# Chunk 0's x in 2 KB pieces ahead of W0, its units in pairs with four turns of the unit matrix before each pair of grams

## The chip, the cores and the metric

One Trainium2 chip, one of its cores. The time is that of the device, in microseconds, from the launch of the program to its end; lower is better. All data are fp32.

## The reference, cut to what matters

```
x = concat([bottom_mlp_output,                       # [2048, 128]
            pairs of einsum('bfd,bgd->bfg', b, b),   # b = bottom_output [2048, 27, 128]; 351 pairs f > g
            zeros], axis=1)                          # [2048, 480]
for w, b in ((w0, b0), (w1, b1), (w2, b2), (w3, b3)):    # 480 -> 1024 -> 1024 -> 512 -> 256
    x = relu(x @ w.T + b)
y = x @ w_out.T + b_out                              # [2048, 1]
```

## The kernel before, in words

The batch is cut into 8 chunks of 256 samples. A chunk has 16 **units** of 16 samples (4 groups of 4). For each sample the gram of its 27 rows of 128 is wanted. TensorE needs the rows turned (dimension in the partitions, tile `xt`), and makes the grams of a unit with 16 small matmuls (`gram`, L614 to 630; the profile counts each twice). A gram is copied from its bank of PSUM into `grams`. When all 16 units of a chunk are there, four DMAs write `grams` to `blocks` in DRAM (the **spill**, L389), and four more (the **gathers**, L394) read the pairs back with a pair in each partition, as the layers need them.

The four layers are products in three parts: a value is split into a high part and the rest (`w_hi`, `w_lo`), and high x high, low x high and high x low are summed. Chunk c has 408 such products of 128x128 by 256 columns (L671), 384 of them in layers 0 to 2. ScalarE drains each result with bias and relu (L763), VectorE and GpSimd split it (L856, L542). ScalarE also makes `w_hi` (L732), the high part of the pairs (L773) and copies grams (L748); VectorE makes `w_lo` (L835).

The order on every engine is written out by `first_steps` (the head, before chunk 0's products) and `chunk_steps`: while chunk c is multiplied, chunk c+1 is prepared at **hooks**, places in the run of products: one each 6 products in chunk 0 (`FIRST_HOOK`), each 36 later. At a hook stand two units (`unit_steps`: VectorE's transposes of the new pair, L844, then the grams of the pair before) and, in chunk 0, groups of four weight tiles that TensorE turns (L597) for layers 1 to 3. Two pairs of the chunk after next are raised ahead as well (`AHEAD`).

For chunk 0 the rows come whole (sample and feature in the partitions, `load_early`, L421 to 424, 448 pieces of 512 bytes for a unit), TensorE turns them with the unit matrix (`turn_early`, L602), ScalarE copies them into `xt` (L740), VectorE copies the gram (L850). Two banks take the turned rows. For all later chunks the rows come by 128-byte pieces in four DMAs a unit (`load_rows`, L426 to 442) into a ring of `ROWS_RING` = 4, and VectorE transposes them in blocks of 32.

Each of the engines works its list in order, and so does SyncE, which issues nearly all DMAs: x of chunk 0 units 0 to 8; the pairs' columns of W0; units 9 to 15; W0's other columns; mlp rows; biases; three of W1's four megabytes; half of chunk 0's spill and gathers (ScalarE issues the other half); W1's last megabyte; rows of chunk 1, units 0 to 3; W2 and W3. Then come the lists of the chunks:

```
sp.wait_ge(mlp_turned, c + 1)
load_mlp(c + 1)
start = isinstance(c, int) and c == 0
for u in range(ROWS_RING if start else ROWS_RING + AHEAD_UNITS, UNITS):
    load_rows(c + 1, u)
...
    for u in range(ROWS_RING):
        load_rows(c + 2, u)
spill(c + 1)
gather(c + 1)
```

A row DMA of unit u waits until the unit that lay in its slot has been transposed. The spill waits until the grams of its chunk are copied. ScalarE's first copy of a gram of the next chunk (`move_gram`, u = 0, L742 to 748) waits until that spill has landed, since `grams` is written again; for chunk 2's first gram this stands in chunk 0's list at product 324. W0's columns for the pairs are put into the gathers' order by GpSimd, 72 copies (L535, L536), and TensorE turns W0 afterwards.

Of the kernel before, what the change touches and what calls it, by code (L numbers as in the profile page):

```python
# [14 lines left out]
P = 128  # L15
# [5 lines left out]
GROUP = 4  # L21
# [6 lines left out]
ROWS_RING = 4  # L28
# [13 lines left out]
BEFORE_CHUNK, LATE_WEIGHTS = ORDER.index(W1_ALL[0]), ORDER.index(W2_ALL[0])  # L42
# [12 lines left out]
ACC_RING, GRAM_RING, TURN_RING = 3, 4, 2  # L55

XT_RING, XT_LAG, UNIT_LAG = 8, 2, 1
# [8 lines left out]
W1_EARLY, FIRST_UNIT, LATE_HOOK = 7, 6, 22  # L66
# [3 lines left out]
EARLY_SLOTS, SHORT_LAG = 8, 2  # L70
# [75 lines left out]
def first_steps():  # L146


    steps = []
    for u in range(UNITS + XT_LAG):  # L150
        if u < UNITS:
            steps.append(("turn", u))
        if 1 <= u <= SHORT_LAG:
            steps.append(("early", u - 1))
        elif u >= XT_LAG + SHORT_LAG:
            steps.append(("early", u - XT_LAG))
    steps += [("spill",), ("mlp",)] + [("weights", n) for n in range(BEFORE_CHUNK)]
    return steps + [("gather",)]


def first_hooks():
# [26 lines left out]
def chunk_steps(now, ahead, first):  # L188
# [47 lines left out]
def dlrm_program(nc, x, x_mlp, w0, b0, w1, b1, w2, b2, w3, b3, w_out, b_out, y):  # L236
    weights = [w0, w1, w2, w3]
    biases = [b0, b1, b2, b3]
    with ExitStack() as ctx:
# [20 lines left out]
        stage_pairs, = shared(("stage_pairs", [P, 8, PAIRS + 1]))  # L260
# [23 lines left out]
        w0_pairs_loaded = sem("w0_pairs_loaded")  # L284
        w0_in_order = sem("w0_in_order")
        w0_dense_loaded = sem("w0_dense_loaded")
# [36 lines left out]
        full_dims = [[DIM, FULL_ROWS], [GROUP * step_n, UNIT_GROUPS], [1, DIM]]  # L323
# [22 lines left out]
        def turned_bank(u):  # L346

            return side_ps if u % TURN_RING else acc[:, ACC_RING - 1]
# [22 lines left out]
        def samples(u):  # L371

            return xt[:, u % XT_RING].rearrange("p j (s f) -> p j s f", s=GROUP)[:, :, :, 0:FEATS]

        def gram_found(u):

            return gram_ps[:, u % GRAM_RING, 0:P].rearrange("p (j f) -> p j f", f=QUAD)[:, :, 0:FEATS]
# [18 lines left out]
        def early_rows_of(u):  # L396

            if u < EARLY_SLOTS:
                return early_rows[:, u]
            u -= EARLY_SLOTS  # L400
            return rows[:, u] if u < ROWS_RING else early_rows[:, u - ROWS_RING]

# [16 lines left out]
        def _(sp):  # L419
            def load_early(u):  # L420
                if u >= EARLY_SLOTS + ROWS_RING:  # L421

                    sp.wait_ge(turned, u - EARLY_SLOTS - ROWS_RING + 1)
# [98 lines left out]
        def _(pool):  # L522
# [9 lines left out]
            pool.wait_ge(w0_pairs_loaded, 16)  # L532
            ordered = raw_rows(0)[:, :, DIM:]
            for col, n, q, step in ROW_RUNS:
                nc.gpsimd.tensor_copy(ordered[:, :, q:q + (n - 1) * step + 1:step], stage_pairs[:, :, col:col + n])  # L535
            nc.gpsimd.tensor_copy(ordered[:, :, PAD_ROW:PAD_ROW + 1], stage_pairs[:, :, PAIRS:]).then_inc(w0_in_order, 1)  # L536
# [23 lines left out]
        def _(pe):  # L560
            def turn_weights(n):
# [5 lines left out]
                elif ring <= n < LATE_WEIGHTS:  # L567
# [11 lines left out]
                if g < W0_GROUPS:  # L579
                    layer, m, part = 0, g, 0  # L580
                    if g == 0:
                        pe.wait_ge(w0_in_order, 1)
                        pe.wait_ge(w0_dense_loaded, 16)
# [11 lines left out]
                for k in range(4):  # L595
                    at = (4 * part + k) * P
                    last = nc.tensor.transpose(bank[:, k * P:(k + 1) * P], src[:, at:at + P], ident[:])  # L597
# [15 lines left out]

            def gram(d, u):  # L614

# [3 lines left out]
                if isinstance(d, int) and d == 1 and u < GRAM_RING:  # L619
                    if u == 0:  # L620

                        pe.wait_ge(w_done, LATE_WEIGHTS)
                elif not (isinstance(d, int) and d == 0 and u < GRAM_RING):

                    pe.wait_ge(grams_done, d * UNITS + u + 1 - GRAM_RING)
                for j in range(UNIT_GROUPS):
                    for s in range(GROUP):
                        at = slice(QUAD * s, QUAD * (s + 1))
                        last = nc.tensor.matmul(gram_found(u)[at, j], xt[:, u % XT_RING, j, at], samples(u)[:, j, s],  # L629
# [316 lines left out]
```

## Time and profile before

| | us |
|---|---|
| median of 3 runs | 509.6 (508.92 to 510.27) |
| the profiled execution | 510.51 |
| its span, on which all rows are | 508.4 |
| TensorE busy | 485.8 |
| VectorE, ScalarE, GpSimd busy | 170.0, 161.6, 132.7 |

All places in time are microseconds from the start of the span. A row of the timeline gives the start, the length and the count of instructions that were merged; the length of a merged row ends with the last of them. PE is TensorE, DVE VectorE, ACT ScalarE, POOL GpSimd, and SPq the queue of SyncE that issues DMAs. Matmuls overlap, so that the distance of two starts tells what one costs. The granted clock of TensorE (PEclk) is 1.00 at 2.4 GHz and 0.50 at 1.2 GHz.

### The profile page before, as it was taken

The numbers are of one execution on the slowest core, as the hardware profiler recorded it, in microseconds if no ns is written. First come the engines' busy times: TensorE is split into PE (matmuls) and PEld (weight loads), VectorE is DVE, ScalarE is ACT, GpSimd is POOL, SyncE is SP. The second block draws the span as 40 slices with busy tenths as digits, with TensorE's granted clock in tenths as the row PEclk, the third lists the DMA queues.
The fourth block names the chain that finished last, engine by engine and source line by source line (L and its number), as shares of the span: only waits on it lengthen the run. The fifth ranks groups of instructions, "written<-read, shape, count | busy, mean of one in ns | idle before, by whom it ended". The sixth has DMA issues, their size and how long they took to land.

```text
span 508.4 us, 18568 instructions
## 1 busy us (share of the span) xinstructions
PE 485.8 (96%) x7595; PEld 467.0 (92%) x7595; DVE 170.0 (33%) x384; ACT 161.6 (32%) x380; POOL 132.7 (26%) x242
## 2 busy tenths in 40 slices
PE   6687967999999999999999999999999999999998
PEld 5576967999999999999999999999999999999997
DVE  1156624444322442134322442144322533131100
ACT  3255523424322342224222332224222432233112
POOL 1530311223312242123222232223222332124221
PEclk9679999999999999999999999999999999999999
DMA  8995876756666556744665556754565564300000
GB/s 219 246 314 143 231 130 100 117 106 123 101 99 121 103 92 108 133 90 77 100 101 113 102 90 95 139 98 68 91 106 125 84 95 72 71 30 2 1 0 1
DMA packets 281091, 53.88 MB, mean 106 GB/s; under 512 B 265126, under 2 KB 279230, under 8 KB 281022
## 3 DMA queue, kind: packets, MB, share of 16 engines
q1 hardware_dynamic: 279090, 52.22, 54.2%
q8 instruction: 60, 0.98, 0.8%
q10 hardware_dynamic: 1932, 0.61, 0.5%
q14 instruction: 9, 0.07, 0.1%
HBM read 45.71 MB, written 7.09 MB: 104 GB/s over the span
## 4 chain that ended last, share of the span: by engine, by line
PE 84%; SPq 8%; DMA 6%; DVE 1%; issue 1%; ACT 0%
PE acc L671 74%; PE gram_ps L629 8%; SPq L442 6%; DMA rows<-in_r_bottom_output_dram 4%; DMA blocks<-grams 2%; SPq L424 1%; PE side_ps L602 1%; PE side_ps L597 1%; PE acc L602 1%; PE side_ps L692 0%; DVE xt L844 0%; SPq L445 0%; SPq L394 0%; PE side_ps L645 0%; PE side_ps L686 0%
## 5 line engine op out<-in xcount | busy, mean ns | idle before, releaser
L671 PE MATMUL acc<-h_a,w_hi 128*128 128x256 f32 x1152 | 221.2, 287 | 0.0
L671 PEld LDWEIGHTS acc<-h_a,w_hi 128*128 128x128 f32 x1152 | 182.9, 191 | 2.2
L763 ACT ACTIVATE h_full<-acc,small_t 128x256 f32<-128x256 f32 x175 | 83.1, 475 | 264.7 <-PE acc L671 264.1
L671 PE MATMUL acc<-h_a,w_lo 128*128 128x256 f32 x576 | 158.6, 283 | 0.0
L542 POOL TENSOR_TENSOR h_a<-h_full,h_a 128x256 fp32r<-128x256 f32 x96 | 72.2, 752 | 175.2 <-DVE h_a L856 175.2
L671 PEld LDWEIGHTS acc<-h_a,w_lo 128*128 128x128 f32 x576 | 110.4, 192 | 0.0
L671 PE MATMUL acc<-x,w_hi 128*128 128x256 f32 x504 | 97.4, 286 | 1.1 <-ACT x L773 1.0
L671 PE MATMUL acc<-h_b,w_hi 128*128 128x256 f32 x512 | 96.8, 285 | 0.0
L542 POOL TENSOR_TENSOR h_b<-h_full,h_b 128x256 fp32r<-128x256 f32 x64 | 47.2, 739 | 179.3 <-DVE h_b L856 179.3
L671 PEld LDWEIGHTS acc<-x,w_hi 128*128 128x128 f32 x504 | 80.5, 191 | 2.3 <-ACT x L773 1.8
L671 PEld LDWEIGHTS acc<-h_b,w_hi 128*128 128x128 f32 x512 | 81.3, 192 | 0.2
L844 DVE STREAM_TRANSPOSE xt<-rows 128x512 f32<-128x512 f32 x112 | 73.5, 690 | 17.1 <-DMA rows<-in_r_bottom_output_dram 16.5
L671 PE MATMUL acc<-x,w_lo 128*128 128x256 f32 x252 | 70.4, 283 | 0.0
L671 PE MATMUL acc<-h_b,w_lo 128*128 128x256 f32 x256 | 70.0, 283 | 0.0
L856 DVE CAST h_a<-h_full 128x256 fp32r<-128x256 f32 x96 | 28.1, 293 | 123.8 <-ACT h_full L763 123.3
L856 DVE CAST h_b<-h_full 128x256 fp32r<-128x256 f32 x64 | 18.6, 292 | 142.3 <-ACT h_full L763 142.3
L629 PEld LDWEIGHTS gram_ps<-xt 128*32 128x32 f32 x4096 | 43.9, 114 | 15.8 <-issue 4.7
L629 PE MATMUL gram_ps<-xt 128*32 128x27 f32 x4096 | 51.8, 199 | 4.7 <-DVE xt L844 2.5
L671 PEld LDWEIGHTS acc<-h_b,w_lo 128*128 128x128 f32 x256 | 49.1, 192 | 0.0
L671 PEld LDWEIGHTS acc<-x,w_lo 128*128 128x128 f32 x252 | 48.3, 192 | 0.0
L748 ACT ACTIVATE grams<-gram_ps 128x108 f32<-128x108 f32 x112 | 36.0, 363 | 35.9 <-PE gram_ps L629 32.3
L597 PE MATMUL gram_ps<-ident,w_raw 128*128 128x128 f32 x96 | 14.1, 282 | 3.7 <-DVE w_lo L835 2.8
(54 smaller groups left out, 178.3 us busy)
## 6 DMA issues: line engine op xcount, KB each, us to landing
rows<-in_r_bottom_output_dram SPq DMA_DIRECT2D x444, 64.0 KB, 2.1
blocks<-grams SPq DMA_DIRECT2D x30, 216.0 KB, 4.0
w_raw<-in_L_rec_w_dram SPq DMA_DIRECT2D x6, 1024.0 KB, 7.5
early_rows<-in_r_bottom_output_dram SPq DMA_DIRECT2D x12, 224.0 KB, 5.9
stage_pairs<-in_L_rec_w_dram SPq DMA_DIRECT2D x1, 1408.0 KB, 11.7
w_raw<-in_L_rec_w_dram SPq DMA_DIRECT2D x2, 512.0 KB, 8.0
mlp_rows<-r_bottom_mlp_output_dram SPq DMA_DIRECT2D x8, 128.0 KB, 2.2
pairs<-blocks SPq DMA_DIRECT2D x8, 126.0 KB
```

Source lines behind the costliest of these rows:

```text
L424: sp.dma_start(early_rows_of(u)[0:FULL_ROWS], x_full[0, u]).then_inc(early_loaded[u], 16)
L442: sp.dma_start(dst, x_blocks[q][d, u]).then_inc(rows_loaded[r], 16)
L542: nc.gpsimd.tensor_tensor(h[:, m, 1, :], h_full[:, slot % 2, :], h[:, m, 0, :].bitcast(F32), ALU.subtract).then_inc(split_done, 1)
L597: last = nc.tensor.transpose(bank[:, k * P:(k + 1) * P], src[:, at:at + P], ident[:])
L602: last = nc.tensor.transpose(turned_bank(u)[:, j * GROUP_ROWS:(j + 1) * GROUP_ROWS], src[0:GROUP_ROWS, j, :], ident[0:GROUP_ROWS, 0:GROUP_ ...
L629: last = nc.tensor.matmul(gram_found(u)[at, j], xt[:, u % XT_RING, j, at], samples(u)[:, j, s], start=True, stop=True, tile_position=(0, Q ...
L671: last = nc.tensor.matmul(acc_slot(c, slot), weight(wp, layer, m, k), in_tile(layer, k, xp), start=(k == 0 and n == 0), stop=(k == K_TILES ...
L748: nc.scalar.activation(gram_place(u), gram_found(u), ACT.Copy).then_inc(grams_done, 1)
L763: nc.scalar.activation(h_full[:, slot % 2, :], acc_slot(c, slot), ACT.Relu, bias=small_t[:, slot:slot + 1]).then_inc(drained, 1)
L844: nc.vector.transpose(xt[:, u % XT_RING].rearrange("p j n -> p (j n)"), rows[:, r].rearrange("p j n -> p (j n)")).then_inc(xt_done, 1)
L856: nc.vector.tensor_copy(h[:, m, 0, :], h_full[:, slot % 2, :]).then_inc(high_done, 1)
```

## The change

- x of chunk 0: the partition now holds four rows that follow each other in DRAM, so that a unit is 112 pieces of 2 KB. All 16 units are issued first, W0 whole (one DMA, 480 columns) behind them. The turned rows come out in another order of columns, which ScalarE's copy (`early_xt`) puts right; `xt` of chunk 0 is now dense, with 27 columns a sample.
- The head goes by pairs of units: two turns, then the grams of the pair before. Ahead of each pair of grams `keep_clock` turns the unit matrix `FILL` = 4 times into the bank of the coming gram. The turned rows have four banks (`TURN_RING`), `xt` four slots instead of eight.
- The row ring has 8 slots instead of 4.
- W1 is issued after the gathers of chunk 0 have landed: its first megabyte, rows of units 0 to 3 of chunk 1, its other three megabytes, rows of units 4 to 7. All groups of W1, W2 and W3 are turned at hooks 2, 4, 6, ... of chunk 0; seven of W1's groups stood ahead of the pairs' products before.
- From chunk 1 on grams use two banks, and the weight groups two others.
- W0 is reordered by GpSimd and VectorE, half of the copies each. ScalarE issues its gathers before it copies weights.

```diff
-ROWS_RING = 4
+ROWS_RING = 8
...
-ACC_RING, GRAM_RING, TURN_RING = 3, 4, 2
-
-XT_RING, XT_LAG, UNIT_LAG = 8, 2, 1
+ACC_RING, GRAM_RING, TURN_RING, UNIT_BANKS = 3, 4, 4, 2
+
+XT_RING, UNIT_LAG = 4, 1
...
-W1_EARLY, FIRST_UNIT, LATE_HOOK = 7, 6, 22
+W1_HOOK, FIRST_UNIT = 2, 6
...
-EARLY_SLOTS, SHORT_LAG = 8, 2
+EARLY_SLOTS, FILL = 8, 4
...
-    for u in range(UNITS + XT_LAG):
+    for u in range(0, UNITS + 2, 2):
         if u < UNITS:
-            steps.append(("turn", u))
-        if 1 <= u <= SHORT_LAG:
-            steps.append(("early", u - 1))
-        elif u >= XT_LAG + SHORT_LAG:
-            steps.append(("early", u - XT_LAG))
-    steps += [("spill",), ("mlp",)] + [("weights", n) for n in range(BEFORE_CHUNK)]
-    return steps + [("gather",)]
+            steps += [("turn", u), ("turn", u + 1)]
+        if u:
+            steps += [("early", u - 2), ("early", u - 1)]
+    return steps + [("spill",), ("gather",), ("mlp",)] + [("weights", n) for n in range(BEFORE_CHUNK)]
...
-    for n in range(BEFORE_CHUNK + W1_EARLY, LATE_WEIGHTS):
-        hooks[n - BEFORE_CHUNK - W1_EARLY].append(("weights", n))
+    for n in range(BEFORE_CHUNK, W_GROUPS):
+        hooks[W1_HOOK + 2 * (n - BEFORE_CHUNK)].append(("weights", n))
...
-    for n in range(LATE_WEIGHTS, W_GROUPS):
-        hooks[LATE_HOOK + 3 * (n - LATE_WEIGHTS)].append(("weights", n))
...
-        steps += [("weights", BEFORE_CHUNK + n) for n in range(W1_EARLY)] + [("pairs", 0)]
+        steps += [("pairs", 0)]
...
-        full_dims = [[DIM, FULL_ROWS], [GROUP * step_n, UNIT_GROUPS], [1, DIM]]
+        full_dims = [[UNIT_GROUPS * DIM, FULL_ROWS], [DIM, UNIT_GROUPS], [1, DIM]]
...
-            return side_ps if u % TURN_RING else acc[:, ACC_RING - 1]
+            return side_ps if u % TURN_RING == ACC_RING else acc[:, u % TURN_RING]
...
-            return gram_ps[:, n % GRAM_RING, :] if n < LATE_WEIGHTS else side_ps[:, :]
+            return gram_ps[:, n % GRAM_RING if n < BEFORE_CHUNK else UNIT_BANKS + n % 2, :]
...
+        def early_xt(u):
+
+            return xt[:, u % XT_RING].rearrange("p j n -> p (j n)")[:, 0:UNIT_COLS].rearrange("p (q h) -> p q h", h=UNIT_GROUPS)
...
-            return turned_bank(u)[:, 0:UNIT_COLS].rearrange("p (j s f) -> p j s f", s=GROUP, f=FEATS)
+            return turned_bank(u)[:, 0:UNIT_COLS].rearrange("p (h q) -> p q h", h=UNIT_GROUPS)
...
-            for u in range(9):
+            for u in range(UNITS):
                 load_early(u)
-            sp.dma_start(stage_pairs[:, :, :], w0_rows[:, :, DIM:]).then_inc(w0_pairs_loaded, 16)
-            for u in range(9, UNITS):
-                load_early(u)
-            sp.dma_start(raw_rows(0)[:, :, 0:DIM], w0_rows[:, :, 0:DIM]).then_inc(w0_dense_loaded, 16)
+            sp.dma_start(stage_w0[:, :, :], w0_rows).then_inc(w0_loaded, 16)
...
-            for i in range(3):
-                load_weights(1, w1, 2 * i, 2 * i + 2, w1_loaded[i])
             spill(0, (0, 1))
             gather(0, PIECES[0::2])
-            load_weights(1, w1, 6, 8, w1_loaded[3])
-            for u in range(ROWS_RING):
+            for t in range(3):
+                sp.wait_ge(gathered[t], 16 * PIECES_OF[t])
+            load_weights(1, w1, 0, 2, w1_loaded[0])
+            for u in range(ROWS_RING // 2):
+                load_rows(1, u)
+            for i in range(1, 4):
+                load_weights(1, w1, 2 * i, 2 * i + 2, w1_loaded[i])
+            for u in range(ROWS_RING // 2, ROWS_RING):
                 load_rows(1, u)
...
-            for col, n, q, step in ROW_RUNS:
+            for col, n, q, step in ROW_RUNS[0::2]:
...
-                    pe.wait_ge(w_done, n)
-                    pe.wait_ge(drained, slot_count(0, ACC_RING))
+                    pe.wait_ge(w_done, n - 1)
...
+            def keep_clock(u):
+
+                for n in range(FILL):
+                    nc.tensor.transpose(gram_ps[:, u % GRAM_RING, (n % 4) * P:(n % 4 + 1) * P], ident[:], ident[:])
+
             def gram(d, u):
+
+                if isinstance(d, int) and d == 0:
+                    if u >= GRAM_RING:
+
+                        pe.wait_ge(grams_done, u + 1 - GRAM_RING)
+                    if u % 2 == 0:
+                        keep_clock(u)
...
+            def order_w0():
+
+                dve.wait_ge(w0_loaded, 16)
+                ordered = raw_rows(0)[:, :, DIM:]
+                for col, n, q, step in ROW_RUNS[1::2]:
+                    last = nc.vector.tensor_copy(ordered[:, :, q:q + (n - 1) * step + 1:step], stage_w0[:, :, DIM + col:DIM + col + n])
+                last.then_inc(w0_in_order, 1)
...
                 if step[0] == "early":
                     early_move(step[1])
+                elif step[0] == "spill":
+                    order_w0()
```

## Rows read from the trace of the kernel before

**Rows 1.** The page: busy time, share of the span and instructions

```profile
PE 485.8 (96%) x7595; PEld 467.0 (92%) x7595; DVE 170.0 (33%) x384; ACT 161.6 (32%) x380; POOL 132.7 (26%) x242
```

**Rows 2.** Stretches: length, TensorE busy (matmuls), granted clock, DMA share, GB/s

```profile
4.20:11.00 6.80, 6.77 (x121) 1.00 1.11 245
11.00:17.80 6.80, 3.40 (x141) 0.99 1.13 300
17.80:24.70 6.90, 5.95 (x144) 0.50 0.97 229
24.70:31.50 6.80, 6.80 (x187) 0.51 0.98 371
```

**Rows 3.** Timeline of the head: start, length, instruction, idle time before it

```profile
4.23 0.95 PE L602 MATMUL acc<-ident,early_rows 108*128 108x108 f32 x4 [4.23 <-DMA early_rows<-in_r_bottom_output_dram]
...
11.38 0.59 PE L602 MATMUL acc<-ident,early_rows 108*128 108x108 f32 x4
...
12.29 0.59 PE L602 MATMUL side_ps<-ident,early_rows 108*128 108x108 f32 x4
...
18.18 11.43 POOL L535 COPY w_raw<-stage_pairs 128x8 f32<-128x8 f32 x71 [15.70 <-DMA stage_pairs<-in_L_rec_w_dram]
...
23.24 0.98 PE L602 MATMUL acc<-ident,early_rows 108*128 108x108 f32 x4
...
24.73 0.98 PE L602 MATMUL side_ps<-ident,early_rows 108*128 108x108 f32 x4
...
33.14 4.45 ACT L732 ACTIVATE w_hi<-gram_ps 128x512 fp32r<-128x512 f32 x8
...
38.60 1.91 PE L597 MATMUL gram_ps<-ident,w_raw 128*128 128x128 f32 x16
...
45.59 0.38 PE L671 MATMUL acc<-x,w_hi 128*128 128x256 f32 x1 [0.99 <-ACT x L773]
```

**Rows 4.** Timeline of SyncE's queue (58.32 twice: to 67.2, and whole)

```profile
30.57 2.29 SPq L389 DMA_DIRECT2D blocks<-grams  x2
39.41 1.67 SPq L394 DMA_DIRECT2D pairs<-blocks  x2
41.12 0.45 SPq L445 DMA_DIRECT2D w_raw<-in_L_rec_w_dram  x1
41.62 14.37 SPq L442 DMA_DIRECT2D rows<-in_r_bottom_output_dram  x16
56.03 1.51 SPq L445 DMA_DIRECT2D w_raw<-in_L_rec_w_dram  x3
...
58.32 9.02 SPq L442 DMA_DIRECT2D rows<-in_r_bottom_output_dram  x6
...
58.32 46.02 SPq L442 DMA_DIRECT2D rows<-in_r_bottom_output_dram  x64
104.38 3.45 SPq L389 DMA_DIRECT2D blocks<-grams  x4
112.21 3.02 SPq L394 DMA_DIRECT2D pairs<-blocks  x4
```

**Rows 5.** Waits (us, times, longest): SyncE 58 to 104.3; VectorE, TensorE 45.5 to 117.7

```profile
SPq L442 <- DVE xt L844: 1.7, 5, 0.5
...
DVE xt L844 <- DMA rows<-in_r_bottom_output_dram: 15.5, 7, 5.9
...
PE side_ps L597 <- DVE w_lo L835: 4.2, 2, 2.5
PE gram_ps L629 <- DVE xt L844: 2.5, 2, 1.6
```

**Rows 6.** Timeline of ScalarE and TensorE where chunk 1 begins

```profile
112.27 0.55 ACT L748 ACTIVATE grams<-gram_ps 128x108 f32<-128x108 f32 x2 [3.67 <-DMA blocks<-grams]
...
117.53 0.28 PE L671 MATMUL acc<-x,w_hi 128*128 128x256 f32 x1
...
117.72 0.42 ACT L773 ACTIVATE x<-pairs 128x256 fp32r<-128x256 f32 x1 [0.19 <-DMA pairs<-blocks]
```

More of the change, by code:

```diff
@@ L41 @@
 ORDER = W0_ALL + SMALL + W1_ALL + W2_ALL + W3_ALL
-BEFORE_CHUNK, LATE_WEIGHTS = ORDER.index(W1_ALL[0]), ORDER.index(W2_ALL[0])
+BEFORE_CHUNK = ORDER.index(W1_ALL[0])
 HIGH, LOW, ALL = (0, 1), (2,), (0, 1, 2)
@@ L258, in dlrm_program @@
         h_full = sb("h_full", [P, 2, CHUNK])
-        stage_pairs, = shared(("stage_pairs", [P, 8, PAIRS + 1]))
+        stage_w0, = shared(("stage_w0", [P, 8, LAYERS[0][0]]))
         _, weighted = shared(("weighted_gap", [P, 5 * 2 * CHUNK]), ("weighted", [P, CHUNK]))
@@ L283, in dlrm_program @@
         small_loaded = sem("small_loaded")
-        w0_pairs_loaded = sem("w0_pairs_loaded")
+        w0_loaded = sem("w0_loaded")
         w0_in_order = sem("w0_in_order")
-        w0_dense_loaded = sem("w0_dense_loaded")
         w1_loaded = [sem(f"w1_loaded{i}") for i in range(4)]
@@ L369, in raw_rows, with samples, gram_found @@
             return w_raw[:, TILE0[n] * P:TILE0[n + 1] * P].rearrange("p (m k) -> p m k", k=k)
[L371 to L377, printed above, removed]
+        def samples(d, u, j, s):
+            if isinstance(d, int) and d == 0:
+                at = GROUP_ROWS * j + FEATS * s
+                return xt[:, u % XT_RING].rearrange("p j n -> p (j n)")[:, at:at + QUAD]
+            return xt[:, u % XT_RING, j, QUAD * s:QUAD * (s + 1)]
+        def early_xt(u):
+            return xt[:, u % XT_RING].rearrange("p j n -> p (j n)")[:, 0:UNIT_COLS].rearrange("p (q h) -> p q h", h=UNIT_GROUPS)
+        def gram_found(d, u):
+            bank = u % GRAM_RING if isinstance(d, int) and d == 0 else u % UNIT_BANKS
+            return gram_ps[:, bank, 0:P].rearrange("p (j f) -> p j f", f=QUAD)[:, :, 0:FEATS]
         def gram_place(u):
@@ L400, in early_rows_of @@
             u -= EARLY_SLOTS
-            return rows[:, u] if u < ROWS_RING else early_rows[:, u - ROWS_RING]
+            return rows[:, u]
         def tile_of_group(g):
@@ L420, in load_early @@
             def load_early(u):
-                if u >= EARLY_SLOTS + ROWS_RING:
-                    sp.wait_ge(turned, u - EARLY_SLOTS - ROWS_RING + 1)
                 sp.dma_start(early_rows_of(u)[0:FULL_ROWS], x_full[0, u]).then_inc(early_loaded[u], 16)
@@ L530, in _ @@
                 nc.gpsimd.memset(raw_rows(0)[:, :, DIM + t * P + n:DIM + (t + 1) * P], 0.0)
[L532 removed]
+            pool.wait_ge(w0_loaded, 16)
             ordered = raw_rows(0)[:, :, DIM:]
[L534 to L536 removed]
+            for col, n, q, step in ROW_RUNS[0::2]:
+                nc.gpsimd.tensor_copy(ordered[:, :, q:q + (n - 1) * step + 1:step], stage_w0[:, :, DIM + col:DIM + col + n])
+            nc.gpsimd.tensor_copy(ordered[:, :, PAD_ROW:PAD_ROW + 1], stage_w0[:, :, DIM + PAIRS:]).then_inc(w0_in_order, 1)
             def split_low(c, layer, m):
@@ L566, in turn_weights @@
                     pe.wait_ge(grams_done, UNITS + 1 - ring + n)
-                elif ring <= n < LATE_WEIGHTS:
+                elif n < BEFORE_CHUNK:
                     pe.wait_ge(w_done, n + 1 - ring)
                 else:
-                    pe.wait_ge(w_done, n)
-                    pe.wait_ge(drained, slot_count(0, ACC_RING))
+                    pe.wait_ge(w_done, n - 1)
                 if g == W0_GROUPS:
@@ L581, in turn_weights @@
                     if g == 0:
-                        pe.wait_ge(w0_in_order, 1)
-                        pe.wait_ge(w0_dense_loaded, 16)
+                        pe.wait_ge(w0_in_order, 2)
+                        pe.wait_ge(w0_loaded, 16)
                 else:
@@ L596, in turn_weights @@
                     at = (4 * part + k) * P
-                    last = nc.tensor.transpose(bank[:, k * P:(k + 1) * P], src[:, at:at + P], ident[:])
+                    cols_k = stage_w0[:, m, 0:DIM] if layer == 0 and k == 0 else src[:, at:at + P]
+                    last = nc.tensor.transpose(bank[:, k * P:(k + 1) * P], cols_k, ident[:])
                 last.then_inc(w_turned, 1)
@@ L612, in turn_early @@
                 turn_rows(u, early_rows_of(u))
+            def keep_clock(u):
+                for n in range(FILL):
+                    nc.tensor.transpose(gram_ps[:, u % GRAM_RING, (n % 4) * P:(n % 4 + 1) * P], ident[:], ident[:])
             def gram(d, u):
+                if isinstance(d, int) and d == 0:
+                    if u >= GRAM_RING:
+                        pe.wait_ge(grams_done, u + 1 - GRAM_RING)
+                    if u % 2 == 0:
+                        keep_clock(u)
+                elif isinstance(d, int) and d == 1 and u < UNIT_BANKS:
+                    if u == 0:
+                        pe.wait_ge(w_done, BEFORE_CHUNK)
+                else:
+                    pe.wait_ge(grams_done, d * UNITS + u + 1 - UNIT_BANKS)
                 pe.wait_ge(xt_done, d * UNITS + u + 1)
@@ L618, in gram @@
                     pe.wait_ge(xt_zeroed, 1)
[L619 to L625, printed above, removed]
                 for j in range(UNIT_GROUPS):
                     for s in range(GROUP):
-                        at = slice(QUAD * s, QUAD * (s + 1))
-                        last = nc.tensor.matmul(gram_found(u)[at, j], xt[:, u % XT_RING, j, at], samples(u)[:, j, s],
+                        at, one = slice(QUAD * s, QUAD * (s + 1)), samples(d, u, j, s)
+                        last = nc.tensor.matmul(gram_found(d, u)[at, j], one, one[:, 0:FEATS],
                                                 start=True, stop=True, tile_position=(0, QUAD * s))
```

8 lines of the change are left out of this document (4 added, 4 removed).

## The prediction

> **What bounds the kernel now.** The page comes first: TensorE is busy for 485.8 us, 96% of the span [rows 1], so what is to be won lies where it is not. The table of stretches [rows 2] shows where that is: 3.40 of 6.80 us between 11.0 and 17.8, and half speed from there to 31.5. That is the head, chunk 0's units and W0, before the products of chunk 0 can start. The timeline of the head [rows 3] shows a unit (turn plus gram) every 0.91 us at 2.4 GHz (11.38 to 12.29) and every 1.49 us at 1.2 GHz (23.24 to 24.73).
>
> After the head one must look at SyncE's queue [rows 4]. It issues everything in written order: chunk 0's spill at 30.57, gathers at 39.41, then from 41.12 to 104.38 W1's last megabyte, 16 row transfers, three issues of W2 and W3, the mlp rows and 64 more row transfers, and only then chunk 1's spill. In 58 to 104 us it waited 1.7 us in all [rows 5]: it is saturated by the issuing itself. Between 45.5 and 117.7 VectorE stood 15.5 us waiting for rows, and TensorE 4.2 and 2.5 us for VectorE [rows 5].
>
> Last, what hangs on chunk 1's spill [rows 6]. ScalarE stood 3.67 us until it had landed (112.2), and converted the third tile of pairs at 117.72, while TensorE's first product of chunk 1 is at 117.53. So chunk 1 starts 13.2 us after its spill is issued (104.38 to 117.53), and the pairs came with hardly any margin. Chunk 0's end is set jointly by TensorE's work and by SyncE's queue. From 117.5 on TensorE is nearly always busy; the sum is therefore made at chunk 1's start.
>
> **The head.** All of x comes before W0, and TensorE finds units 8 to 15 landed: in the 512-byte pieces of before, 245 GB/s were moved in 4.2 to 11.0, and 371 GB/s when W1's longer pieces ran in 24.7 to 31.5 [rows 2]. One unit is 229 KB, 0.94 us at the first rate, 0.62 at the second; both are less than what a unit costs TensorE with its fill (below), or about equal, so TensorE sets the pace. Fill: 16 turns of 128x128 took 1.91 us [rows 3], 0.12 each, so four are 0.48 us at 2.4 GHz and 0.95 at 1.2. A pair of units costs 2x0.91+0.48 = 2.30 us, or 2x1.49+0.95 = 3.93 us. The first turn is at 4.23. The matmuls of 4.2 to 11.0 ran at the lower level too: the column says 1.00, but the first unit's four turns took 0.95 us as those at 23.24 did (0.98), and 0.59 at 11.38. TensorE had been busy for 6.77 of those 6.80 us. I take the same rise at 11.0: 6.8/3.93 = 1.7 pairs until then, 6.3 pairs x 2.30 = 14.4 us after it, 25.4, and 0.4 for the last copy: spill at 25.8 instead of 30.57. Bounds: 23.0 if the clock is up from the start (8x2.30), 28.6 if it rises only at 17.8, 36.0 if never (8x3.93).
>
> The spill took 8.84 us (30.57 to 39.41) beside three megabytes of W1, and 7.83 us from one queue in chunk 1 (104.38 to 112.21) [rows 4]. Now W1 is gone from beside it and two queues issue: 7.6, between 5.9 (a third less) and 8.8. It lands at 33.4. The gathers: ScalarE read the first tile 3.05 us after their issue and the last 5.5 us after it in chunk 1, beside row transfers [rows 4, 6]; alone and over two queues I take 3.5 (3.0 to 4.5): 36.9.
>
> W0 lands behind x (5.6 MB at 300 to 371 GB/s, 16 to 20 us). Its reordering, 71 copies in 11.43 us on GpSimd [rows 3], becomes 35 or 36 of them there (5.8 us, done at some 26) and the rest on VectorE behind its last gram copy. Those 35 copies aren't in the trace: at GpSimd's 0.16 us each they end at 31.5, under the spill's landing. Cost nothing; were the spill's cover gone it would be up to 5.7 us. ScalarE now waits for the spill, issues its gathers (some 1.9 us), then copies the mlp tile and nine weight groups, 4.45 us for eight [rows 3]: products with pairs can start at some 40.3 instead of 45.59 [rows 3]. W1's seven groups, turned while TensorE had nothing else, now lie among the products: 7x0.48 = 3.3 us. If TensorE were the only limit, that would be the whole of it.
>
> **The queue.** SyncE now waits until the gathers have landed (36.9) and goes on where it went on at 41.12 before: 4.2 us earlier. What stands ahead of chunk 1's spill grows by two things.
> - Sixteen row transfers more. With a ring of eight, units 0 to 7 of chunk 2 are written ahead of chunk 1's spill, where units 0 to 3 were; each is four issues. The 64 transfers of 58.32 to 104.34 took 46.02 us, 5.3 of it for W2 and W3 (next point) and 1.7 waiting: 0.61 us each. 16x0.61 = 9.8 us (16x0.53 = 8.5 at the least; 16x0.90 = 14.4 as in the 14.37 us from 41.62).
> - Three megabytes of W1, issued in the head before, now behind it. Right after W2 and W3 (2.5 MB) six row transfers took 9.02 us where 3.7 is normal [rows 4]: 5.3 us, 2.1 per MB; with 0.5 for each issue 3x2.6 = 7.9 us (1.5, the issues alone, to 9).
> The ring of eight takes away the 1.7 us of waiting. From 41.12 to 104.38 it was 63.3 us; now 63.3+9.8+7.9-1.7 = 79.3. So chunk 1's spill is issued at 36.9+79.3 = 116.2 instead of 104.38, 11.8 us later. The rows of chunk 1's own units gain nothing either: their queue starts 4.2 us earlier and has 7.9 us more of W1 in it.
>
> Does TensorE get there sooner? Products from 40.3; at the tenth hook (60 products on) it needs W1's second megabyte, issued behind 16 row transfers at some 37.4+14.4 = 51.8 and landed near 56, while TensorE is there near 49.5 (60x0.12 and four groups of 0.48 after 40.3): a stop of 6 to 7 us. Units come at the pace of their rows. At product 324 ScalarE meets the gram of chunk 2 that waits for the spill, and everything it drains afterwards stands behind that wait, where it stood 3.67 us before. TensorE can fill three accumulators, then it stops, until 116.2+7.8. From there the order is that of before, so chunk 1 starts at 116.2+13.2 = 129.4, 11.8 us after 117.5.
>
> In the later chunks the same 64 row transfers lie between two spills as before: 7.83 until the gathers' issue, 3.02 for that [rows 4] and 64x0.61 = 39 make 50 us, and seven chunks share 508.4-117.5, 56 us each. So the queue doesn't lose more there, and what chunk 0 lost isn't made good. The rings of two gram banks and four xt buffers there cost nothing: a pair is raised while the pair before it is multiplied; with that cover gone, a copy of 0.3 us per unit.
>
> **Sum.** Profiled execution 510.5 us (span 508.4 and 2.1 around it) + 11.8 = 522.3; the median of the runs is 0.9 under the profiled one: 509.6+11.8 = 521.4, and I say 521. The ends: head 5 us less or 5 more, queue 7.8 less (71.5) or 7 more. The forecast's own range is 513 to 528.
>
> **A rule on the clock.** The rows show the clock at 0.50 from 17.8 to 31.5, with TensorE busy 5.95 of 6.90 us and then 6.80 of 6.80 [rows 2]; at 38.60 turns of 0.12 us show it up again [rows 3], and it was up at 11.0 after 24 turns and three units' grams. So a stretch full of turns was followed by a rise, and I count the fill as activity. The Trainium skill, TensorE: Matmul & The Clock Gate, Part 4 (PE-mode transpose), says that work in transpose mode does not count as busy for the clock gate. By that rule the fill only costs, which is rival 2; by the rows it helps.
>
> **Rivals.**
> 1. TensorE, not SyncE's queue, sets chunk 1's start; the weights hide behind row issues. It would decide if chunk 1's spill were issued within 67.5 us of 36.9, that is by 104.4, against 79.3 in my sum. Then: 5.3 us earlier start, 3.3 back for W1's groups, 7.7 us of stops gone (4.2 for w_lo, 2.5 for xt [rows 5] and 1.0 for the pairs at 45.59 [rows 3]), 6.5 for the new stop at W1: 3.2 us faster, 506.4; without that stop 500. For it: the head gains for certain, and in 11.0 to 31.5 transfers and weights ran side by side at 229 to 371 GB/s [rows 2]. Against it: 1.7 us of waiting in 46 us of issuing. Chance 0.18.
> 2. The clock stays at 1.2 GHz in the head, since turns don't count or since four are too few: spill at 36.0, 10.2 us later than forecast, 531. Against it: 6.77 of 6.80 us busy sufficed at 11.0, and pairs leave fewer gaps. Chance 0.08.
> 3. The change doesn't do what it says in one respect: W1's price is hidden but not the rows': 79.3-6.4 = 72.9, 514. Chance 0.04; that all of it cancels to within 0.3%, 0.04.
>
> **How the numbers follow.** Forecast 0.66, and 0.12 for the other two slower ones: slower 0.78, the same 0.04 (0.3%, about 1.5 us, is what a measurement of this kernel can tell), faster 0.18. The range from 512 to 529 takes in the forecast's own, rival 3 and half-way cases to rival 2; it leaves out rival 1 and most of rival 2.
>
> **What would show it.** Right: chunk 0's first spill near 26; the granted clock up from about 11 to at least 26; in SyncE's queue 96 row transfers between W1's first megabyte and the spill of chunk 1, that spill at 112 to 120; ScalarE's wait for it many us instead of 3.67; TensorE idle before chunk 1's first product, near 129; a stop at W1's second megabyte near 50. Wrong: the spill of chunk 1 at or before 104, row transfers issued at 0.53 each with the weights in between costing nothing, or a head at half speed.

## The result and the profile after

The changed kernel takes 523.74 us (median of 4 runs, 522.55 to 527.75) against 509.26 for the kernel before on the same chip: ratio 1.0304, 95% interval 1.0264 to 1.0343, slower by 14.5 us. The forecast was 521 (11.8 us slower), with a range of 512 to 529. The profiled execution is the slowest of the four, 527.75 us with a span of 526.0, so its places in time are some 4 us late against the median.

The page, busy time (against [rows 1]):

```profile
PE 492.1 (94%) x7627; PEld 475.4 (90%) x7627; DVE 172.1 (33%) x419; ACT 160.8 (31%) x380; POOL 126.8 (24%) x207
```

TensorE is busy 6.3 us more in a span that is 17.6 us longer (the rows of the fill, the extra turns of the unit matrix, are 6.1 us); the rest is standing still. The timeline of SyncE's queue, which answers to [rows 4]:

```profile
33.07 1.39 SPq L391 DMA_DIRECT2D blocks<-grams  x2
39.88 1.65 SPq L396 DMA_DIRECT2D pairs<-blocks  x2
45.38 0.41 SPq L444 DMA_DIRECT2D w_raw<-in_L_rec_w_dram  x1
45.83 11.09 SPq L441 DMA_DIRECT2D rows<-in_r_bottom_output_dram  x16
56.96 1.51 SPq L444 DMA_DIRECT2D w_raw<-in_L_rec_w_dram  x3
58.52 16.23 SPq L441 DMA_DIRECT2D rows<-in_r_bottom_output_dram  x16
74.79 1.51 SPq L444 DMA_DIRECT2D w_raw<-in_L_rec_w_dram  x3
76.35 0.98 SPq L462 DMA_DIRECT2D mlp_rows<-r_bottom_mlp_output_dram  x1
77.37 44.70 SPq L441 DMA_DIRECT2D rows<-in_r_bottom_output_dram  x64
122.12 3.49 SPq L391 DMA_DIRECT2D blocks<-grams  x4
```

All 96 row transfers stand between W1's first megabyte and the spill of chunk 1. That spill is issued at 122.12, where it was 104.38. The queue waited only 1.4 us for free slots on the way. The chain of work that ended last runs over this queue up to the spill, so chunk 1 hangs on it. The timelines of ScalarE and TensorE there (against [rows 6]):

```profile
128.93 0.53 ACT L760 ACTIVATE grams<-gram_ps 128x108 f32<-128x108 f32 x2 [12.20 <-DMA blocks<-grams]
...
130.09 0.58 PE L683 MATMUL acc<-h_a,w_hi 128*128 128x256 f32 x1 [6.67 <-DVE h_a L876]
...
134.52 0.41 PE L683 MATMUL acc<-x,w_hi 128*128 128x256 f32 x1
```

What TensorE waited for in 45 to 135 (us, times, longest):

```profile
PE acc L683 <- DVE h_a L876: 6.7, 1, 6.7
PE gram_ps L597 <- DMA w_raw<-in_L_rec_w_dram: 4.4, 1, 4.4
PE gram_ps L641 <- DVE xt L856: 1.4, 1, 1.4
```

ScalarE stood 12.20 us (3.67 before) at the gram that may only be moved when the spill has landed. TensorE filled its accumulators, reached layer 3 and stopped for 6.67 us; the name in the row is VectorE's, which waited for ScalarE's drains. The 4.4 us are the stop at W1's second megabyte. Chunk 1 begins at 134.52, 17.0 us after 117.53. From there to the end it is 391.5 us (390.9 before), and 390.7 to 391.4 in every version below: whatever a version gains or loses is settled before chunk 1 starts.

The stretches of the head, with their granted clock (against [rows 2]):

```profile
4.20:11.00 6.80, 5.30 (x85) 1.00 0.99 262
11.00:17.80 6.80, 4.73 (x136) 1.00 1.06 270
17.80:24.70 6.90, 5.49 (x133) 0.75 0.63 236
24.70:31.50 6.80, 5.90 (x252) 1.00 0.03 6
```

The clock is at 2.4 GHz for 17 of the head's 29 us: the turns and grams up to 13.0 still took as long as those at 1.2 GHz (0.98 us for four turns, whatever the column says), and the column shows 0.50 from 19.8 to 23.2. TensorE has gaps at either level. The first spill comes at 33.07, not at 25.8, and even 2.5 us after that of the kernel before. And x in 2 KB pieces moved at 262 GB/s in the first stretch, against 245 at 512 bytes.

One execution is a coarse measure of a head. e1_spill_ahead, below, has the same head instruction for instruction, and there the first spill came 2.2 us earlier:

```profile
30.87 1.68 SPq L391 DMA_DIRECT2D blocks<-grams  x2
```

So a difference of some 2 us between the heads of two single executions shows nothing.

### The profile page after: what moved, and what is told of

The parts are those of the page before. It is cut to its first block, busy times and chain, and to the rows that moved or that the text cites. A ratio compares the mean times of both kernels' runs of the same rounds, so it can differ in the third digit from the quotient of the medians.

```text
span 526.0 us, 18616 instructions
## 1 busy us (share of the span) xinstructions
PE 492.1 (94%) x7627; PEld 475.4 (90%) x7627; DVE 172.1 (33%) x419; ACT 160.8 (31%) x380; POOL 126.8 (24%) x207
## 4 chain that ended last, share of the span: by engine, by line
PE 81%; SPq 10%; DMA 5%; issue 2%; DVE 1%; ACT 0%; ACTq 0%; DVEq 0%
PE acc L683 69%; SPq L441 9%; PE gram_ps L641 8%; DMA blocks<-grams 2%; DMA early_rows<-in_r_bottom_output_dram 1%; DMA rows<-in_r_bottom_output_dram 1%; PE acc L602 1%; PE gram_ps L617 1%; DMA pairs<-blocks 1%; PE gram_ps L597 1%; SPq L444 1%; SPq L391 1%; PE side_ps L602 0%; PE side_ps L704 0%; DVE xt L856 0%
## 5 line engine op out<-in xcount | busy, mean ns | idle before, releaser
L683 PE MATMUL acc<-h_a,w_hi 128*128 128x256 f32 x1152 | 224.5, 289 | 6.7 <-DVE h_a L876 6.7
L683 PEld LDWEIGHTS acc<-h_a,w_hi 128*128 128x128 f32 x1152 | 184.9, 193 | 8.9 <-DVE h_a L876 6.9
L542 POOL TENSOR_TENSOR h_b<-h_full,h_b 128x256 fp32r<-128x256 f32 x64 | 47.1, 737 | 178.2 <-DVE h_b L876 178.2
L683 PEld LDWEIGHTS acc<-x,w_hi 128*128 128x128 f32 x504 | 82.0, 195 | 0.6
L641 PEld LDWEIGHTS gram_ps<-xt 128*32 128x32 f32 x4096 | 42.9, 112 | 15.7 <-issue 6.0
L641 PE MATMUL gram_ps<-xt 128*32 128x27 f32 x4096 | 50.1, 197 | 5.9 <-issue 4.5
L760 ACT ACTIVATE grams<-gram_ps 128x108 f32<-128x108 f32 x112 | 35.9, 363 | 38.2 <-PE gram_ps L641 25.8
L847 DVE TENSOR_TENSOR w_lo<-gram_ps,w_hi 128x512 fp32r<-128x512 f32 x34 | 23.0, 686 | 23.6 <-ACT w_hi L744 23.6
## 6 DMA issues: line engine op xcount, KB each, us to landing
stage_w<-in_L_rec_w_dram SPq DMA_DIRECT2D x1, 1920.0 KB, 14.5
```

The source lines that it names most:

```text
L542: nc.gpsimd.tensor_tensor(h[:, m, 1, :], h_full[:, slot % 2, :], h[:, m, 0, :].bitcast(F32), ALU.subtract).then_inc(split_done, 1)
L641: last = nc.tensor.matmul(gram_found(d, u)[at, j], one, one[:, 0:FEATS], start=True, stop=True, tile_position=(0, QUAD * s))
L683: last = nc.tensor.matmul(acc_slot(c, slot), weight(wp, layer, m, k), in_tile(layer, k, xp), start=(k == 0 and n == 0), stop=(k == K_TILES ...
L760: nc.scalar.activation(gram_place(u), gram_found(d, u), ACT.Copy).then_inc(grams_done, 1)
L847: last = nc.vector.tensor_tensor(w_lo[:, a:b], bank, w_hi[:, a:b].bitcast(F32), ALU.subtract)
```

## The experiments

All are timed beside the kernel before, which had 508.7 to 508.9 us as the median of those comparisons. The sizes below are differences of medians to it: +14.5 for the changed kernel.

### Which part of the queue's order costs what

**e1_spill_ahead.**

```diff
                 if more:
-                    for u in range(ROWS_RING):
+                    for u in range(ROWS_RING // 2):
                         load_rows(c + 2, u)
                 spill(c + 1)
                 gather(c + 1)
                 if more:
-                    for u in range(ROWS_RING, ROWS_RING + AHEAD_UNITS):
+                    for u in range(ROWS_RING // 2, ROWS_RING + AHEAD_UNITS):
```

> The changed kernel with one thing moved: in each chunk's list on SyncE the spill and the gathers of the next chunk stand behind rows of units 0 to 3 of the chunk after it, as before the change, and units 4 to 7 come after them. Theory (SyncE's queue sets chunk 1's start): 16 row transfers at 0.54 to 0.61 us leave the way of the spill, which is issued 9 to 10 us earlier, near 113; chunk 1's first product comes near 126, where TensorE's own work ends (it stood at 123.3 with 24 products to go), and its clock has no long stop to fall in: 9 us faster than the changed kernel, 514 to 516. Rival (TensorE's work or the rows of chunk 1 set it): within 2 us of the changed kernel.

517.55 us, ratio 1.0180 (1.0137 to 1.0222): +8.8. SyncE's queue there:

```profile
75.58 34.99 SPq L441 DMA_DIRECT2D rows<-in_r_bottom_output_dram  x48
110.62 3.38 SPq L391 DMA_DIRECT2D blocks<-grams  x4
```

The spill comes at 110.6 and chunk 1 starts at 124.2. From W1's first issue (43.33) to the spill it is 67.3 us, 9.4 less than the changed kernel's 76.7, so the 16 transfers cost the queue what was expected. The gain of the whole is 6 us rather than 9, and the chain that ended last shows why. The last transfer on it is one of chunk 1's rows, landed at 87.2; after that it stays nearly all with TensorE until chunk 1 begins, and the spill isn't on it:

```profile
84.96 2.28 DMA rows<-in_r_bottom_output_dram
...
116.11 9.94 PE acc L683 x80
```

With the queue this much shorter, TensorE's own work ends last. The profiled execution of the changed kernel, from which the 9 was read, was also 4 us over its median. The rival (within 2 us) is out.

**e2_w1_in_head.**

```diff
+            for i in range(3):
+                load_weights(1, w1, 2 * i, 2 * i + 2, w1_loaded[i])
             spill(0, (0, 1))
...
-            load_weights(1, w1, 0, 2, w1_loaded[0])
-            for u in range(ROWS_RING // 2):
-                load_rows(1, u)
-            for i in range(1, 4):
-                load_weights(1, w1, 2 * i, 2 * i + 2, w1_loaded[i])
-            for u in range(ROWS_RING // 2, ROWS_RING):
+            load_weights(1, w1, 6, 8, w1_loaded[3])
+            for u in range(ROWS_RING):
                 load_rows(1, u)
```

> The changed kernel with three megabytes of W1 issued in the head again, the last one after the gathers; all else as changed. Theory (queue): 3 MB at 2.1 us and three issues of 0.5 leave the way of chunk 1's spill: issued 7 to 8 us earlier, near 114.5; less what the spill of chunk 0 loses beside W1 in the head (up to 1.3 us). TensorE's stop of 4.4 us for W1's second megabyte goes. In all 6 to 8 us faster than the changed kernel, 516 to 518. Rival (the price of the weights is hidden behind the issuing of rows, only the 16 row transfers count): within 2 us.

520.52 us, ratio 1.0240 (1.0197 to 1.0283): +11.8, so 3 us gained of 6 to 8; the interval overlaps that of the changed kernel slightly.

```profile
34.91 1.93 SPq L391 DMA_DIRECT2D blocks<-grams  x2
...
46.80 0.39 SPq L444 DMA_DIRECT2D w_raw<-in_L_rec_w_dram  x1
47.24 20.80 SPq L441 DMA_DIRECT2D rows<-in_r_bottom_output_dram  x32
...
114.31 3.41 SPq L391 DMA_DIRECT2D blocks<-grams  x4
```

From W1's first issue behind the gathers to chunk 1's spill it is 67.5 us, 9.2 less than the changed kernel's 76.7; 7.9 was the price. But the first spill is at 34.9, later than in either execution of the changed head (33.07 and 30.87). What W1 gives the queue it takes in part in the head, not by slowing the spill (34.91 to 41.16) but earlier: TensorE's unexplained stops were 6.5 us in all, 5.2 in the changed kernel and 3.8 in e1 (see below).

**e3_both** is e1 and e2 together.

> Both edits at once: the order of SyncE's queue is that of before again, with x ahead of W0, 2 KB pieces, the ring of eight and the fill left in. Theory: the two parts add up, chunk 1's spill is issued near 106 and chunk 1 starts at 119 to 120: 14 to 15.5 us faster than the changed kernel, 508.5 to 511, level with the kernel before. Rival (the slow head with its late first spill and the hooks carry a part of the loss of their own): 513 or more.

512.87 us, ratio 1.0078 (1.0053 to 1.0103): +4.1. The two parts give 5.7 and 2.7 apart and 10.4 together, of 14.5: within the noise of each, about 2 us, they add up. The queue's order is more than two thirds of the loss. The expectation of a level result was wrong by 2 to 4 us, as its rival said; what is left isn't in the queue's order, and the head is where it was looked for. From W1's last megabyte to the spill:

```profile
47.25 0.40 SPq L444 DMA_DIRECT2D w_raw<-in_L_rec_w_dram  x1
...
106.59 3.41 SPq L391 DMA_DIRECT2D blocks<-grams  x4
```

With e1 and e2 beside it, the queue's 76.7 us can be told apart: 59.3 us for what stood in it before, 8.2 (e2 less e3) to 9.4 (changed kernel less e1) for the 16 transfers, 8.0 (e1 less e3) to 9.2 (changed kernel less e2) for the three megabytes of W1.

**e6_before_ring8** puts the same cause into the kernel before. To make room it also halves the slots of `xt`.

```diff
-ROWS_RING = 4
+ROWS_RING = 8
...
-XT_RING, XT_LAG, UNIT_LAG = 8, 2, 1
+XT_RING, XT_LAG, UNIT_LAG = 4, 2, 1
```

> The kernel before with a ring of eight row slots and four xt slots (for room), nothing else. Its list on SyncE then has units 0 to 7 of chunk 2 ahead of chunk 1's spill instead of 0 to 3. Theory: 16 row transfers at 0.61 us, less 1.7 us of waits that the ring takes away: the spill of chunk 1 at 111.5 to 113 instead of 104.4, and the whole 7 to 8.5 us slower, 516 to 517.5. Rival (the ring costs nothing by itself, it was the late head that made the queue late): within 1.5 us of the kernel before.

517.76 us, ratio 1.0171 (1.0151 to 1.0191): +8.9. Its SyncE queue:

```profile
41.28 22.82 SPq L442 DMA_DIRECT2D rows<-in_r_bottom_output_dram  x32
64.14 2.73 SPq L445 DMA_DIRECT2D w_raw<-in_L_rec_w_dram  x3
...
67.89 43.95 SPq L442 DMA_DIRECT2D rows<-in_r_bottom_output_dram  x64
111.89 3.43 SPq L389 DMA_DIRECT2D blocks<-grams  x4
```

ScalarE's timeline where chunk 1 begins:

```profile
118.61 0.53 ACT L748 ACTIVATE grams<-gram_ps 128x108 f32<-128x108 f32 x2 [11.10 <-DMA blocks<-grams]
```

With the head of before and W1 where it was, the larger ring makes chunk 1's spill 7.5 us late and the kernel 8.9 us slower. Sixteen more transfers took 22.82-14.37 = 8.5 us [rows 4], 0.53 each. The fewer slots of `xt` weren't timed alone, but nothing points at them: the queue got to W1's last megabyte 0.35 us earlier than before, and from there to the spill it waited 1.4 us for VectorE, against 1.7. This is the clearest of the runs: a deeper ring is a longer list ahead of the spill, because the list was written ring by ring.

### The head: fill, clock, and stops that nothing explains

**e4_no_fill** sets FILL to 0. 

> The changed kernel without the fill (none instead of four turns of the unit matrix ahead of a pair of grams; no result depends on them). Theory (the fill counts as activity and holds the clock, but the head's lateness is TensorE standing still for nothing that the profile shows, some 5 us): without it the granted clock stays at 0.50 for longer in the first 33 us, eight fills of 0.48 to 0.95 us fall away, and the two about cancel: chunk 0's spill at 31 to 35, the whole within 2 us of the changed kernel. Rival 1 (turns don't count for the clock, so the fill is only work): clock as with it, spill 4 to 6 us earlier, near 28, and as much faster. Rival 2 (the fill is what holds the clock, and all hangs on it): spill at 37 or later, 4 us slower.

521.49 us, ratio 1.0250 (1.0199 to 1.0302): +12.8, by the medians 2 us faster than with the fill, though the intervals overlap, and the first spill at 30.08 (33.07 and 30.87 with it). Stretches of the head:

```profile
11.00:17.80 6.80, 3.74 (x121) 0.84 1.06 288
17.80:24.70 6.90, 5.60 (x147) 0.50 0.55 200
24.70:31.50 6.80, 5.29 (x206) 0.66 0.02 5
```

The clock falls at 15.7 and is back at 29.3; with the fill it was at 0.50 from 19.8 to 23.2, and in e1, with the same head, from 16.9 to 23.7. So the stretch at half speed was 13.7 us without the fill and 3.4 or 6.8 with it. The fill shortens it, and still doesn't pay.

**e11_fill_doubled** sets FILL to 8. 

> The changed kernel with eight turns instead of four. Theory (once the clock is up a fill is only work): 32 turns more at 0.12 to 0.24 us, 4 to 7 us of TensorE in the head, of which the clock gives back at most the 3.4 us of the stretch at 0.50; chunk 0's spill near 36 and the whole 1 to 4 us slower than the changed kernel. Rival (more activity pays): the granted clock stays up through the whole head and the whole is no slower.

526.42 us, ratio 1.0347 (1.0307 to 1.0386): +17.7. The first spill was at 33.10, not near 36. The clock was at 0.50 for 6.8 us, no less than with four turns in e1, and at 1.00 from 24.7 on. The whole is 2.7 us slower than the changed kernel, inside what was expected of it. Zero, four and eight turns give +12.8, +14.5 and +17.7: each four cost some 2 to 3 us. The intervals of neighbours overlap, those of zero and eight don't. Where the eight lose theirs isn't settled, since only one execution of each was profiled.

**The stops.** In the changed kernel's chain of waits through the head, in order of time:

```profile
15.18 0.55 PE gram_ps L641 x42
15.73 2.67 issue
18.41 0.33 PE gram_ps L641 x16
...
23.82 0.80 issue
...
27.96 0.75 issue
...
31.35 1.00 issue
```

"issue" is time in which the engine waited for nothing that the profile shows. These four come in the middle of a run of grams or turns, 5.2 us in all, and the long one is the one that falls while x and W0 are being moved; the three short ones fall when the transfers have ended (0.03 DMA share in 24.7 to 31.5). The page lists a DMA queue of its own for instructions, 60 packets; in the trace packets of 16 KB start at 15.7, 22.2, 25.9 and 29.8, each 2.4 to 2.8 us ahead of a stop's end. The packet itself takes 1.0 to 1.3 us each time, also at the long stop: what differs is how late it starts. That made the theory: TensorE runs out of instructions, and their load stands behind the data in the same 16 DMA engines. The stops also belong to places in the program and not to times. The first leaves 16 records of grams in the changed kernel, e1, e2, e3, e7 and e8 alike, at 16.3 to 18.4; the third leaves two turns in all of these but e1.

**e5_x_gated** keeps few transfers in flight.

```diff
             def load_early(u):
+                if u >= 4:
+                    sp.wait_ge(turned, u - 3)
```

> The changed kernel, in which SyncE issues chunk 0's unit u from 4 on only when unit u-4 has been turned, so that few row transfers are in flight in the head; W0 then comes behind them, later. Looked at is only the head. Theory (the stops of TensorE after which the profile names nothing, 2.7 us at 15.7 and 0.8 to 1.0 us later, are loads of TensorE's own instructions, which queue behind the data in the same DMA engines): with the engines nearly free the first of them shrinks from 2.7 to at most 1.2 us. Rival (they have nothing to do with the data in flight): it stays at 2.5 to 3.3 us. The whole is no faster than the changed kernel, since W0 is later.

One execution, 522.11 us. The rows of TensorE's timeline in the head that end such a stop:

```profile
18.09 0.61 PE L643 MATMUL gram_ps<-xt 128*32 128x27 f32 x43 [0.65 <-issue]
...
23.52 0.49 PE L604 MATMUL side_ps<-ident,rows 108*128 108x108 f32 x2 [2.05 <-issue]
...
27.82 0.31 PE L643 MATMUL gram_ps<-xt 128*32 128x27 f32 x11 [0.26 <-issue]
```

No stop is left in 14 to 17 us, and the second, at 17.4, is 0.65 us. The stop of 2.05 us isn't the first one moved: it stands at the place of the third, with two turns left, which was 0.75 us in the changed kernel with the engines idle and now has W0 under way (DMA share 1.00 in 21.4 to 23.5). Where W1 is in the head, the same place cost 2.9 to 3.2 us in e2, e3, e7 and e8:

```profile
30.43 0.34 PE L600 MATMUL side_ps<-ident,rows 108*128 108x108 f32 x2 [3.23 <-issue]
```

The first spill is at 28.54, 2.3 to 4.5 us earlier than in the two executions of the changed head, though nothing was taken from TensorE's work. So the first and the third stop were long with data in flight and short or gone without it. The second hardly moved: 0.80 us in the changed kernel, and 1.0 to 1.1 in e2, e3, e7 and e8 with the engines full (DMA share 1.02 to 1.06 in 21 to 24). And e11, with more turns between the grams, had none after the first. That the stops are instruction loads is read from the packets' times and from these fixed places, and wasn't tested by itself. It fits the late heads of e2 and e3.

### Towards a version that beats both

**e7_no_gather_wait** is e3 without SyncE's wait for chunk 0's gathers.

```diff
-            for t in range(3):
-                sp.wait_ge(gathered[t], 16 * PIECES_OF[t])
```

> As e3_both (the order of the queue as before the change), and SyncE doesn't wait until chunk 0's gathers have landed before it goes on. That wait was 5.6 us less 1.7 of issuing. Theory: SyncE goes on 3.9 us earlier, near 43.3; the gathers share the engines with W1's last megabyte, but ScalarE reads the pairs only at 49.3; chunk 1's spill near 103 instead of 106.6: 3 to 4 us faster than e3_both where the queue sets the end, 509 to 510. Rival (TensorE, whose products with pairs start at 50.3 there, sets it by now): within 1.5 us of e3_both.

512.42 us, ratio 1.0070 (1.0048 to 1.0092): +3.6, so nothing beyond the noise against e3. The spill of chunk 1 came at 103.90 instead of 106.59, but ScalarE no longer waited for it (3.8 us in e3), and from 60 us on the chain that ended last is nearly all TensorE's: the rival.

**e8_w1_early** adds to e7 the order of before on ScalarE and TensorE.

```diff
-    return steps + [("spill",), ("gather",), ("mlp",)] + [("weights", n) for n in range(BEFORE_CHUNK)]
+    return steps + [("spill",), ("mlp",)] + [("weights", n) for n in range(BEFORE_CHUNK)] + [("gather",)]
...
-        steps += [("pairs", 0)]
+        steps += [("weights", BEFORE_CHUNK + n) for n in range(W1_EARLY)] + [("pairs", 0)]
```

> As e7_no_gather_wait, and ScalarE issues its gathers behind the nine weight groups again, and seven groups of W1 are turned ahead of the pairs' products, as before the change. TensorE and ScalarE work while the spill and the gathers are under way: products with pairs near 47 instead of 50.3 and 3.3 us less of weight turns among them. Theory: TensorE's part gets 5 to 6 us shorter; with the queue's 3.9 us from e7_no_gather_wait, 505 to 508, the first version that is faster than the kernel before. Rival (ScalarE's half of the gathers comes late, or the queue alone sets the end): no faster than e7_no_gather_wait.

511.34 us, ratio 1.0052 (1.0027 to 1.0077): +2.5. Too much was hoped for: 5 to 6 us of TensorE's part gave one, inside the noise. Chunk 1's spill now waited 2.9 us for its grams, so the queue was ahead of TensorE.

**e9_w1_early_no_fill** is e8 with FILL at 0. 

> As e8_w1_early without the fill. There chunk 1's spill waited 2.9 us for its grams, so TensorE's side sets the end by now. Theory (the fill buys clock but costs what it buys; without it, in e4_no_fill, the first spill came 3 us earlier and the whole was 2.2 us faster): spill of chunk 0 at 30.5 to 32 instead of 33.5, 1 to 3 us faster than e8_w1_early, 508.5 to 510.5. Rival (the fill is worth its time, e4_no_fill was a lucky phase of the clock): 511 or more.

509.00 us, ratio 0.9998 (0.9977 to 1.0018), level with the kernel before, 2.3 us faster than e8, with intervals apart: this is the pair that shows that the fill costs, and by about what the medians gave in e4. TensorE stood 7.8 us in three such stops in its head, with 2 KB pieces, W0 and W1 all issued at once:

```profile
PE gram_ps L637 <- issue: 7.8, 3, 4.0
```

**e10_also_gated** is e9 with unit u of chunk 0, from 5 on, issued when u-4 units have been turned (by the edit; that is unit u-5). 

> As e9_w1_early_no_fill, and unit u of chunk 0 from 5 on is issued only when unit u-4 has been turned. Theory (instruction loads queue behind data): TensorE's stop near 14 goes from some 3 us to under 1; but W0 and three megabytes of W1 now run in 18 to 30 us and the later stops stand in their way, and W0 lands near 27 instead of 23, so that GpSimd's half of it is ready near 33. Spill of chunk 0 near 29, W0 turned from 33 on; 507.5 to 510. Rival (W0's lateness costs what the head gains): within 1 us of e9_w1_early_no_fill or slower.

507.36 us, ratio 0.9968 (0.9946 to 0.9989; 12 runs against 23): 1.4 us faster than the kernel before, the only version that beats both. Its stops in the head:

```profile
17.71 0.40 PE L639 MATMUL gram_ps<-xt 128*32 128x27 f32 x25 [0.90 <-issue]
...
24.64 1.65 PE L639 MATMUL gram_ps<-xt 128*32 128x27 f32 x108 [3.75 <-issue]
```

The first is short, the second, with W0 and W1 in flight behind the units, is as long as ever. The first spill is at 26.72. Against e9 alone the intervals overlap, so that the gate's own worth isn't settled.

## Why the prediction was right, and where it was not

- **SyncE's queue sets chunk 1's start: right.** The forecast was 79.3 us from W1's first issue to chunk 1's spill; it was 76.7. The spill came at 122.12, outside the 112 to 120 that was to show it, because the queue started late. Of the terms, 16 row transfers, 9.8 us less 1.7, were 8.2 to 9.4, and three megabytes of W1, 7.9, were 8.0 to 9.2. The 63.3 us taken over from before were 59.3 in e3, 3.9 too many; why the same list went faster there isn't shown. The 1.7 us of waiting that the ring was to take away were still 1.4.
- **Chunk 1 follows its spill by 13.2 us: right.** It was 12.4, with ScalarE's wait in the place and TensorE's stop for its drains as described. That TensorE's clock would fall in that stop (0.51 in 129 to 136) wasn't foreseen.
- **TensorE's stop at W1's second megabyte: right**, 4.4 us for 6 to 7, and covered in the changed kernel as said. In e1, with the queue shorter, it is on the chain.
- **The head: wrong by 7.3 us** (33.07 for 25.8). The step that failed is "TensorE sets the pace", with 2.30 us for each pair. It had two faults. The kernel before showed a stop in the midst of a unit's grams:

```profile
15.49 0.26 PE L629 MATMUL gram_ps<-xt 128*32 128x27 f32 x6 [2.25 <-issue]
```

  The sum has no term for it. It isn't a wait for x; x ahead of W0 doesn't remove it, and such stops recur, 5.2 us in all. And x at 2 KB was priced at up to 371 GB/s, a rate of W1's 4 KB pieces; at 262 GB/s TensorE stood 1.5 us for units 2 and 3. The rest is the clock, at 1.2 GHz until 13.0 and in 19.8 to 23.2. At 7.3 us the miss is larger than the 5 that the sum allowed the head.
- **The wait for the gathers** was 5.5 us for 3.5 (39.88 to 45.38), over its upper bound of 4.5; the spill 6.8 for 7.6. The pairs, which were to be ready for products at 40.3, were converted by ScalarE from 47.6 on.
- **The errors cancelled in part, and that is luck.** Head and gathers were 8.5 us too early, the queue 2.6 and the last step 0.8 too long. The sum was 11.8; measured were 14.5 by medians and 17.0 at chunk 1's start in the profiled execution. The cause that was forecast holds; that the number lies within 3 us owes something to errors of opposite sign.
- **The clock.** The prediction counted turns as activity, and the changed kernel shows it more plainly than the fill does. From 33.4 the clock was at 0.50, TensorE did nothing but 16 turns of weights from 36.3 to 39.9, and at 40.3 the clock rose:

```profile
33.50:40.00 6.50, 3.64 (x16) 0.50 0.68 140
40.50:43.50 3.00, 0.00 (x1) 1.00 0.30 80
```

  The Trainium skill, TensorE: Matmul & The Clock Gate, Part 4, says that transposes don't count as busy; these rows speak against it. But the conclusion drawn, that a fill which holds the clock helps, was wrong: by e8 and e9 it costs 2 us. What was also not foreseen is that TensorE, idle while the spill and the gathers are under way, would have its clock at 0.50 in 33.4 to 40.3 and in 43.7 to 47.1, where it was at 1.00 before.
- **Rival 1 (TensorE sets the end)** is out for the changed kernel, and true of e7 to e10, whose queue is short enough. Rival 2 (half speed in the whole head) is out by the 1.00 in 13.0 to 19.8 and from 23.2 on, though its other half, a fill that only costs, came true by another way than turns that don't count. Rival 3 (W1's price hidden) is out by e2's 9.2 us.

## What to carry to other kernels

In a queue that issues in written order, look for what the next stage waits for (here a spill of 3.5 us) and count what stands ahead of it; a ring made deeper moves its prefetches ahead of it too, and here the deeper ring cost 9 us in a kernel that was otherwise as before (e6). Once such a queue is short enough, the next limit, here TensorE, takes over, and further cuts give less than they free (e1, e7). A stop with nothing behind it in the middle of a run of instructions wasn't a wait for x here, and at two places of the program it was longer with more data in flight. Work that only keeps the clock up must be weighed against the time at the lower clock that it saves: here four turns a pair took 6.1 us of TensorE, shortened the stretch at half speed from 13.7 us to 3.4 or 6.8, and lost.

## What the runs showed of the hardware

- In 4.2 to 11.0, with x under way in 229 KB transfers, 2 KB pieces moved at 262 GB/s in the changed kernel and at 272 to 304 in the eight others that issue all of x at once; 512-byte pieces moved at 245, and at 242 in e6. A quarter of the descriptors gave between 7 and 26% more. It isn't the size of the pieces that held x there: W0, in pieces of 1,920 bytes, was moved at 374 GB/s in 17.8 to 22.0. What held it stays open.
- A row transfer of 512 pieces of 128 bytes mostly followed the one before by 0.53 us on the issuing queue. A few took much longer, the longest right behind W1 or W2 and W3, and they bring the mean of a run of them to 0.6 to 1.1. So the issuing alone sets the rate only where no large transfer is just ahead. Behind W1's other three megabytes:

```profile
59.41 4.80 SPq L441 DMA_DIRECT2D rows<-in_r_bottom_output_dram  x2
```

- TensorE's stops without a releaser in a run of grams or turns lasted 0.3 to 1.3 us with the DMA engines idle. With x, W0 or W1 in flight the first and the third stop lasted 1.8 to 4.0 us, the second 0.7 to 1.1 (0.9 and 2.0 in e10 and e9, without the fill), and one was gone.
- The clock rose at 40.3 in the changed kernel after TensorE had done nothing but 16 turns since 33.4.
